# Rotary embedding in a decoder layer: the sine products go to GpSimd by way of ScalarE, the cosine products stay on VectorE

## What is computed

```python
def rotary_apply(x, cos, sin):
    d = x.shape[-1]
    x1, x2 = (x[..., :d // 2], x[..., d // 2:])
    c, s = (cos[..., :d // 2], sin[..., :d // 2])
    return jnp.concatenate([x1 * c - x2 * s, x2 * c + x1 * s], axis=-1)
...
q = rotary_apply(jnp.transpose(q, (0, 2, 1, 3)), cos, sin)
k = rotary_apply(jnp.transpose(k, (0, 2, 1, 3)), cos, sin)
...
x = x + attention(layernorm(x))
x = x + scan(ctx, z=layernorm(x))        # state step: state * exp(d_t * A) + d_t * u_t * B_t
x = x + ffn(layernorm(x))                # bitlinear, gelu, bitlinear
```

## Time and profile before

| | |
|---|---|
| time, median of 3 runs | 969.58 us (968.82 to 969.89) |
| the profiled execution | 975.44 us, its span 973.6 us |
| TensorE busy | 898.5 us, 92% |
| VectorE busy | 854.6 us, 88% |
| ScalarE busy | 735.7 us, 76% |
| GpSimd busy | 615.3 us, 63% |
| granted TensorE clock, mean | 0.972 of full speed |
| TensorE, VectorE busy from 0 to 25 us | 16.49 and 12.73 us |
| filler transposes (L1708) | 190 |

### The profile page before, as it was taken

How to read it: one execution, slowest core, us unless ns; L and a number is a source line. 1 busy time by engine, 2 the same in 40 slices (tenths; PEclk the granted TensorE clock), 3 DMA queues, 4 the chain that set the end, 5 groups by cost and what they waited for, 6 DMA issues and landing times.

```text
span 973.6 us, 17249 instructions
## 1 busy us (share of the span) xinstructions
PE 898.5 (92%) x5426; PEld 589.9 (61%) x5426; DVE 854.6 (88%) x1167; ACT 735.7 (76%) x1476; POOL 615.3 (63%) x439
## 2 busy tenths in 40 slices
PE   6998779789999999989999999789899999999998
PEld 5465546556776666677756678667755455544544
DVE  4599999999999979899998999999989989998741
ACT  5888955935757996776988776796589999999551
POOL 1277854655347638892663999525679879878620
PEclk9999898899999999999999999799999999999999
DMA  6668848778757655173635645642137566755283
GB/s 224 219 219 272 225 125 243 180 205 215 224 144 202 170 177 153 63 209 108 180 99 145 205 116 180 238 110 93 55 61 176 122 135 128 149 109 125 59 165 80
DMA packets 146296, 153.55 MB, mean 158 GB/s; under 512 B 90448, under 2 KB 94800, under 8 KB 145952
## 3 DMA queue, kind: packets, MB, share of 16 engines
q1 hardware_dynamic: 146208, 152.45, 58.1%
HBM read 103.00 MB, written 28.44 MB: 135 GB/s over the span
## 4 chain that ended last, share of the span: by engine, by line
PE 46%; ACT 16%; DVE 15%; issue 11%; POOL 10%; DMA 1%; ACTq 0%; DVEq 0%; POOLq 0%; SPq 0%
PE ps L1765 8%; PE ps L1834 7%; PE ps L1891 6%; PE ps L1808 4%; DVE hb L1911 4%; POOL hb L1382 4%; PE ps L1881 4%; PE ps L1778 3%; ACT ps L1502 3%; ACT p_q L1615 3%; PE ps L1846 3%; DVE y_acc L1933 2%; PE ps L1820 2%; PE ps L1789 2%; PE ps L1739 2%
## 5 line engine op out<-in xcount | busy, mean ns | idle before, releaser
L1382 POOL TENSOR_TENSOR hb<-du,b_bc 128x1024 f32<-128x1024 f32 (+1 forms) x160 | 308.0, 1949 | 95.8 <-PE ps L1834 90.8
L1911 DVE TENSOR_TENSOR_SCAN hb<-ps,hb 128x1024 f32<-128x1024 f32 (+1 forms) x128 | 256.7, 2012 | 16.0 <-ACT ps L1502 12.3
L1502 ACT ACTIVATE ps<-delta,a_neg 128x511 f32<-128x511 f32 (+2 forms) x320 | 179.4, 598 | 87.1 <-DVE hb L1911 82.8
L1933 DVE SCALAR_TENSOR_TENSOR y_acc<-ps,ct,y_acc 128x512 f32<-128x512 f32 x256 | 178.7, 736 | 15.8 <-PE ps L1834 15.2
L1834 PE MATMUL ps<-ident,hb 128*128 128x128 f32 x1088 | 151.5, 282 | 24.6 <-DVE hb L1911 8.1
L1834 PEld LDWEIGHTS ps<-ident,hb 128*128 128x128 f32 x1088 | 124.9, 144 | 55.1 <-issue 16.3
L1615 ACT ACTIVATE p_q<-ps,m_col 128x512 f32<-128x512 f32 (+3 forms) x256 | 131.8, 536 | 10.2 <-DVE m_col L2008 9.2
L1765 PE MATMUL ps<-xn_t,w_ring 128*128 128x512 f32 x256 | 121.1, 618 | 0.9 <-ACT p_t L1631 0.6
L1881 PE MATMUL ps<-t_fc,xt 128*128 128x512 f16 x512 | 117.6, 381 | 0.8 <-ACT h_sb L1679 0.8
L1891 PE MATMUL ps<-t_pr,ht 128*128 128x512 f16 x512 | 113.0, 379 | 0.5 <-DMA ht<-hs 0.5
L1631 ACT ACTIVATE p_t<-ps 128x512 f32<-128x512 f32 x160 | 86.4, 611 | 30.1 <-PE ps L1808 29.8
(11 more groups left out here) (137 smaller groups left out, 1500.0 us busy)
## 6 DMA issues: line engine op xcount, KB each, us to landing
w_ring<-in_w_attn SPq DMA_DIRECT2D x32, 512.0 KB, 4.8
qk_d<-hl SPq DMA_DIRECT2D x64, 256.0 KB
q_st<-qk_d SPq DMA_DIRECT2D x64, 256.0 KB, 4.3
b_bc<-bc_d SPq DMA_DIRECT2D x48, 256.0 KB, 4.6
raw<-in_w_fc SPq DMA_DIRECT2D x16, 512.0 KB, 4.3
raw<-in_w_pr SPq DMA_DIRECT2D x16, 512.0 KB, 5.2
k_st<-qk_d SPq DMA_DIRECT2D x32, 256.0 KB, 4.7
k_st<-qk_d SPq DMA_DIRECT2D x64, 128.0 KB, 4.7
```

The source lines that it names most:

```text
L1382: nc.gpsimd.tensor_tensor(piece_of(e, hi, lo).rearrange("p (a n) -> p a n", a=2), du[b % 2][:, 2 * h:2 * h + 2, lo:hi], b_bc[:, i % BC_RIN ...
L1502: ins = nc.scalar.activation(factors(j, hi, lo)[:, (hi - lo) * m + start:(hi - lo) * (m + 1)], delta[b % 2][:, et, lo + start:hi], ACT.Exp ...
L1911: v.tensor_tensor_scan(h, d, h, 0.0, ALU.mult, ALU.add).then_inc(scan_done, 1)
L1933: v.scalar_tensor_tensor(out=y, in0=bank(kind, r, tb), scalar=ct[:, b % 2, tb, n:n + 1], in1=y, op0=ALU.mult, op1=ALU.add).then_inc(y_free ...
```

## The change

ScalarE copies each half of the rotation out of its PSUM bank, into part 2 or 3 of `hl`. GpSimd multiplies these two parts by the sine in place, and then adds and subtracts as before. VectorE reads each bank once, for the cosine product. Two semaphores are new, `rot_out` (a half is copied) and `rot_sin` (a half is multiplied). The wait for `hl_stored` moves with the first write from VectorE to ScalarE. VectorE's product waits for the copy (`rot_out`), GpSimd's products for both copies, and the bank is free after VectorE's product, which comes behind the copy. `follows` has the new shares, and all tables of due times hold new numbers.

```diff
 WEIGHT, SLOT_AT, STATE_AT, ... (all tables of due times and weights)
-SLOT_AT = [-70.63, -1.1, -20.34, 0.54, 115.31, 113.43, 78.09, 84.3, 153.3, 152.56, 215.37, 144.34, 186.75, 225.59, 239.97,
+SLOT_AT = [-104.31, -181.71, -66.38, -18.1, 144.93, 65.53, -17.21, 90.52, 113.24, 192.67, 215.91, 112.47, 239.96, 136.22,
...
     elif kind == "rot":
         b, n, half = a
         yield "pe", 3.45, [act("ln1b", b, LT - 1), sp("wload", CHUNK_OF[kind, b, n])]
-        yield "dve", 1.2, [pe(*item)] + ([dve("rot", b, n, 0)] if half else [sp("lo", *divmod(4 * b + n - 1, 4))] if b or n > 1 else [])
+        yield "act", 0.5, [pe(*item)] + ([act("rot", b, n, 0)] if half else [sp("lo", *divmod(4 * b + n - 1, 4))] if b or n > 1 else [])
+        yield "dve", 0.6, [act(*item)]
         if half:
-            yield "pool", 2.46, [dve(*item)]
+            yield "pool", 4.9, [dve(*item)]
...
-            readers = ("act", "dve") if kind == "inproj" else (reader,)
+            readers = ("act", "dve") if kind in ("inproj", "rot") else (reader,)
...
                     b, n, _ = a
                     turned = turned_of(b, n)
+                    consts(pool, "rotary")
+                    pool.wait_ge(rot_out, 8 * b + 2 * n + 2)
+                    for half in range(2):
+                        nc.gpsimd.tensor_tensor(turned[:, 2 + half, :], turned[:, 2 + half, :], sin[:], ALU.mult)\
+                            .then_inc(rot_sin, 1)
                     emptied(pool, TASK[(kind, *a)])
+                    pool.wait_ge(rot_sin, 8 * b + 2 * n + 2)
                     nc.gpsimd.tensor_tensor(turned[:, 0, :], turned[:, 0, :], turned[:, 3, :], ALU.subtract)
                     nc.gpsimd.tensor_tensor(turned[:, 1, :], turned[:, 1, :], turned[:, 2, :], ALU.add).then_inc(rot_done, 1)
...
+                elif kind == "rot":
+
+                    b, n, half = a
+                    act.wait_ge(m_full, TASK[(kind, *a)] + 1)
+                    if half == 0 and (b or n > 1):
+                        act.wait_ge(hl_stored, 64 * (4 * b + n))
+                    nc.scalar.activation(turned_of(b, n)[:, 2 + half, :], bank(kind, *a), ACT.Copy).then_inc(rot_out, 1)
...
-                elif kind == "rot" and a[2] == 0:
-                    b, n, _ = a
-                    task = TASK[(kind, *a)]
-                    src, turned = bank(kind, *a), turned_of(b, n)
+                elif kind == "rot":
+                    b, n, half = a
                     consts(dve, "rotary")
-                    if b or n > 1:
-                        dve.wait_ge(hl_stored, 64 * (4 * b + n))
-                    dve.wait_ge(m_full, task + 1)
-                    own.done(v.tensor_tensor(turned[:, 0, :], src, cos[:], ALU.mult))
-                    v.tensor_tensor(turned[:, 2, :], src, sin[:], ALU.mult).then_inc(m_free["dve"], 1)
-                elif kind == "rot":
-                    b, n, _ = a
-                    task = TASK[(kind, *a)]
-                    src, turned = bank(kind, *a), turned_of(b, n)
-                    dve.wait_ge(m_full, task + 1)
-                    v.tensor_tensor(turned[:, 3, :], src, sin[:], ALU.mult)
-                    v.tensor_tensor(turned[:, 1, :], src, cos[:], ALU.mult).then_inc(m_free["dve"], 1)
+                    dve.wait_ge(rot_out, 8 * b + 2 * n + half + 1)
+                    v.tensor_tensor(turned_of(b, n)[:, half, :], bank(kind, *a), cos[:], ALU.mult).then_inc(m_free["dve"], 1)
```

More of the change, by code:

```diff
@@ new lines @@
+SSM_AT = [-3.91, 282.05, 406.3, 671.37]
+SSM_DONE = [201.0, 410.69, 1005.03, 708.93]
+TILE_AT = [406.78, 698.19, 719.21, 779.92, 739.89, 696.56, 745.04, 789.79, 686.57, 833.34, 763.51, 939.5, 922.01, 1042.83,
+ 915.9, 854.51]
+STATE = [{'exp': [321.55, 64.12],
+  'dbu': [251.24, 482.95],
+  'scan': [-395.11, -55.49],
+  'ht': [-58.92, -60.06, -12.41, 32.16]},
+ {'exp': [267.66, 266.71],
+  'dbu': [-221.75, -380.62],
+  'scan': [176.18, 231.86],
+  'ht': [-39.73, -12.11, 18.84, 28.49]},
+ {'exp': [-73.79, 0.65],
+  'dbu': [-101.86, -134.23],
+  'scan': [-457.36, -51.65],
+  'ht': [-153.51, -243.34, -57.45, -29.73]}]
@@ new lines @@
+LAST_STATE = {'exp': [74.96, 28.92],
+ 'dbu': [-257.35, -282.11],
+ 'scan': [-154.34, -343.04],
+ 'carry': [-303.98, -12.22],
+ 'ht': [-424.29, -23.0]}
+LAST_ROWS = [-221.53, -283.21, -206.05, -413.58, -196.65, -331.12, -112.13, -139.34, 15.52, -159.72, -57.16, -100.93, -218.03,
+ 83.03, -154.83, -150.5, -262.92, -21.88, -170.69, 24.31, 26.15, -106.94, -267.63, 40.48, 78.25, -73.03, -98.62,
+ -68.17, 203.27, 11.54, 32.38, -71.66]
+LAST_END = {'gate': [327.16, 183.64, -151.59, 87.55],
+ 'gt': [-82.1, 192.91, 6.87, -27.59, 119.31, 279.19, 316.17, 99.41],
+ 'xadd': [-113.05, 154.34, 154.83, 5.81]}
@@ L395 @@
+TILE = {'fxload': [9.51],
+ 'xa': [-92.93],
+ 'xc': [30.48],
+ 'xt': [-208.19],
+ 'fc': [159.51, 34.21, 50.63, 132.17],
+ 'hstat': [-261.0],
+ 'hn': [-422.61, -382.24],
+ 'ht_ffn': [-213.25, 39.26],
+ 'proj': [67.69]}
+FIRST_TILE = {'xa': [-27.38], 'xc': [-2.84]}
+SWITCH = 59.78
 PATIENCE = 0.18
@@ L1029, in layer_kernel @@
         lo_ready = sem("lo_ready")
+        rot_out = sem("rot_out")
+        rot_sin = sem("rot_sin")
         rot_done = sem("rot_done")
```

484 lines of the change are left out of this document (225 added, 259 removed), and 12 rows, old and new, of tables (ATTN_END, SKIP).

## The result

The changed kernel takes 988.26 us (median; 987.09 to 988.44) where the kernel before takes 969.74 us on the same chip: a ratio of 1.0185, 95% interval 1.0169 to 1.02. It is 18.5 us slower; forecast were 961.7 us and a range of 953 to 976.

What follows compares the result with a forecast made beforehand. No engine was taken as the bound alone; VectorE set the pace from 125 to 350 us. Relief 12.9 - 4.0 - 1.0 = 7.9 us gain, from 969.58 to a median of 961.7 us, range 953 to 976.

Steps and rivals of the forecast that it cites:

- Part one: VectorE loses 32 sine products of 0.60 us, 19.2 us in all; counted by stretch, a gain of 12.9 us.
- Parts two and three: ScalarE gains 32 copies and table loads (24.0 us), GpSimd 32 products (41.0 us); half of 3.8 + 4.1, about 4.0 us lost.
- Part four: VectorE held up by GpSimd at the ternary product with two SBUF operands: 15% of 6.8 us, 1.0 us lost.
- The rival of a VectorE that is stopped generally: Each GpSimd sine product stops VectorE for its whole length: 28.1 us slower, 997.7 us; chance 3%.
- Part five: Newly planned order: 21 more filler transposes on TensorE costed at nothing; scatter of a few microseconds left to the range.
- The rotation itself becomes the late one, at GpSimd: Rival: GpSimd's longer part of the rotation delays the heads' load and TensorE's scores: 6.5 us slower, 976.1 us; chance 22%.
- The signs named for "wrong": VectorE idle growing as its work falls, above all scans waiting; GpSimd products before scores; stretched SBUF instructions; change after 700.
- after 700: From 700 us on, feed-forward tiles share the core with the last scans; no change of time expected there.

Runs made afterwards that it cites:

- products_added: Kernel before, its order held, with 32 more GpSimd sine products in the rotation ahead of its sums; VectorE keeps both products: 995.76 us, 27.0 us slower.
- products_elsewhere: Kernel before, its order held, with 32 more GpSimd products outside the rotation, ahead of every third product for the scans: 981.76 us, 12.3 us slower.
- hi_later: products_added with ScalarE's rounded copy of the rotated parts (`hi`) put 2.56 us later in ScalarE's queue: 984.65 us, 16.2 us slower than the kernel before.
- old_order_hi_later: old_order with `hi` put 2.56 us later in ScalarE's queue, the copies not moved: 982.88 us, ratio 1.0148 to the kernel before.
- old_order_no_sine: old_order without GpSimd's 32 sine products, the sine left out and ScalarE's copies kept: 970.53 us, 1.8 us slower than the kernel before.
- old_order: Changed rotation with the queue order, banks and filler transposes of the kernel before held: 990.03 us, 20.5 us slower than the kernel before.
- no_sine: Changed kernel in its new order without GpSimd's 32 sine products, ScalarE's copies kept: 979.42 us, 9.9 us slower than the kernel before.

## Why the prediction was wrong

**Part one, VectorE's relief: near in size.** 12.9 us were forecast; alone it is worth 9.9, GpSimd's shorter sums included, and 17.7 with the copies in place (988.2 to 970.5).

**Parts two and three: the step that failed.** The middle of "hidden" and "priced by the chain share", 4.0 us, stood for what costs 30.4 in the held order (11.7 and 18.7). Two things were wrong in it. The share of the chain tells where the chain runs now, and is no price: put 41 us on GpSimd and its share goes from 10% to 21% in `products_added` and to 19% in `products_elsewhere`, at 27.0 and 12.3 us, while it stays at 10% in the changed kernel. And the waits were looked for in the wrong place. The prediction named ScalarE's new wait at the copy and left it at nothing because it cost VectorE 2.0 us; on ScalarE it is 17.6 to 23.5. It asked who waits for the rotation's result, and named SyncE's load and TensorE's scores; the first to wait is `hi` on ScalarE, and behind it in the queue the exponentials, for which TensorE waits. Behind the copy, the prediction had named the decay factors and the transposed probabilities. The row of `hi` stood in the trace of before, 4.4 us in three waits, small only because GpSimd was mostly in time. Moving `hi` alone, every instruction the same, brought 10.8 us back in `hi_later` (27.0 to 16.2) and 6.0 in `old_order_hi_later` (20.5 to 14.5). About half of the cost stays when the load stands outside the rotation (16.7 of 30.4 us), so load on engines that are busy 63% and 76% was not hidden either. Through which waits that half is lost is not shown, beyond the rows beside those runs.

**Part four: right for the held order, short by seven in the new one.** In the held order GpSimd's products lengthen VectorE's work by 0.8 us (busy 835.1 in `old_order_no_sine`, 835.9 in `old_order`), where 1.0 was priced. In the new order they lengthen it by 7.7 (836.1 in `no_sine`, 843.8 in the changed kernel). So VectorE's busy time fell by 18.7 us in `old_order`, as the 19.2 removed, but by 10.8 in the changed kernel. In the same queue without the products (`no_sine`) three lines are shorter:

```profile
L2085 DVE SCALAR_TENSOR_TENSOR tern<-raw,thr,low 128x1024 f16<-128x1024 f32 x16 | 25.6, 1602 | 0.6
...
L1965 DVE TENSOR_SCALAR x_in<-x_in,mv,rstd 128x512 f32<-128x512 f32 x16 | 14.3, 902 | 0.9 <-POOL rstd L1444 0.9
...
L2050 DVE SCALAR_TENSOR_TENSOR nmr<-mv,rstd 128x4 f32<-128x4 f32 x4 | 2.7, 669 | 0.0
```

The products add 3.6 us to the ternary product, 3.0 to the normalized x and 2.1 to `nmr`; what the last two grew by beyond that (3.3 and 2.1, from 11.0 and 0.6 before) came with the order. The rival of a VectorE that is stopped generally is refuted by the scans: 2281 ns in the mean, 2280 before. The page "SBUF — State Buffer" of the Trainium skill, section "Who interferes with whom", has VectorE instructions with two inputs in SBUF share a port with GpSimd that one of them holds alone, while one with a single SBUF input goes free outside the two-port modes. The trace agrees in the first kind, `nmr` (146 to 1204 ns in the mean) and the ternary product (1602 to 1825 with the products), and in the scan, which has one. The normalized x (696 to 1093 ns) has one too; whether it runs in a two-port mode no run shows.

**Part five: the second step that failed.** The new order was costed at nothing with "a few microseconds to either side". With the rotation of before it is 19.6 us slower. It did what it could be planned for: `hi` waits 0.9 us in it instead of 28.1, VectorE's cosine 5.1 instead of 24.9. But the copy stands 23.5 us for TensorE, and the order gave away elsewhere what it won: 988.3 against 990.0 in the held order. Which of its rows lose the 19.6 us was not taken apart and stays open, and so does whether a better order for this rotation exists. Which step weighs more depends on the path: order first, it costs 19.6 us, and the rotation within it comes out even (relief and copies gain 9.6, the products cost 8.6); rotation first, it costs 20.5, and the order gives 2.0 back. The runs do not choose between the paths, and the scatter shows only that one trial of an order says little.

**The rivals.** "The rotation itself becomes the late one, at GpSimd" had the direction and the late result at GpSimd, with 6.5 us and 22%, but SyncE's load and TensorE's scores as those who wait. It counted the three places where the chain of before ran through GpSimd's part; the wait at `hi` in `products_added` came in all 16 rotations.

**What would show it.** ScalarE's and GpSimd's work grew about as said (21.0 and 45.3 us, forecast 24 and 41). The signs named for "wrong" came: scans waiting for factors and products grew from 15.1 to 33.0 us (to 25.9 by the new order alone), and VectorE's idle time rose from 119.0 to 141.5 us (span less busy time) while its work fell by 10.8 where about 21 was said. Nothing changed after 700, as said.

## What to carry to other kernels

Work that is added inside a chain of hand-overs between in-order queues should be priced by its own load and by who stands still at the next hand-over and what is queued behind, rotation by rotation, not by an engine's share of the chain or its idle time; the row to look for is the short wait that is small only because the supplier is early. Moving the waiting instruction later in its own queue is a cheap test, and here gave back three to four tenths of the loss. Where a planner sets the order, a new plan for the same work can land tens of microseconds away (969 and 1025 here), so a change that needs one should be measured in the old order too.
